# One core, Mamba layer: sums of the decay, C·B products and a logarithm moved within a pipelined step

## The reference, cut to what matters

```python
o = silu(depthwise3x3(lin1(x)))
s = o @ fc_in                                   # [b, l, 32]
z, xBC, dt = split(s @ W_in)
xs, B, C = split(silu(causal_conv4(xBC)))
dt = softplus(dt + dt_bias); dA = exp(-dt * exp(A_log))
h = dA_t * h + (dt_t * x_t) * B_t;  y_t = h @ C_t      # forward; and again on the flipped sequence
y = (y + D * xs) * silu(z)
y = y * rsqrt(mean(y * y, -1) + 1e-5) * norm_w
out = y @ W_out                                 # both directions are added, then fc_out, norm, gate
```

## Time and profile before

| what | value |
|---|---|
| median of 3 runs | 9643.34 us |
| profiled execution, its own time | 9645.11 us |
| its span | 9643.3 us |
| mean granted TensorE clock in it | 0.879 of full |
| TensorE / VectorE / ScalarE busy over the span | 76% / 69% / 60% |
| Mamba layer in the span | about 1933 to 2860 us |
| steps 17 to 31 (all three groups of blocks) | from about 2135 to 2465 us |
| steps 32 to 40 (no convolution) | from about 2468 to 2668 us |
| steps 41 to 48 (only q) | from about 2668 to 2799 us |

### The profile page before, as it was taken

The page is one execution under the profiler, slowest core; times in us unless marked ns, Lnnn a source line. Parts: engine busy times, 40 slices in busy tenths (PEclk is TensorE's granted clock), DMA queues, the critical chain, the costliest instruction groups (busy, mean ns, idle before and its releaser), DMA issues. The chain is left out here.

```text
span 9643.3 us, 117031 instructions
## 1 busy us (share of the span) xinstructions
PE 7297.0 (76%) x37876; PEld 2493.7 (26%) x37876; DVE 6652.7 (69%) x10617; ACT 5742.5 (60%) x4945; POOL 1957.9 (20%) x1578
## 2 busy tenths in 40 slices
PE   8999999968860998487666676666666676666787
PEld 3333333234430333322211122111211122111422
DVE  6777777767557333566677777877777777877565
ACT  3222232136535222322799988999799988999432
POOL 5655666400012000133000000000000000000133
PEclk9999999978875999588899998999899999999687
DMA  1000000001100000000000000000000000000000
GB/s 43 1 1 1 1 1 1 2 24 25 25 1 6 0 0 0 2 0 0 1 1 1 0 1 1 0 0 0 1 1 0 0 1 1 0 1 0 3 0 35
DMA packets 26732, 43.17 MB, mean 4 GB/s; under 512 B 13451, under 2 KB 16653, under 8 KB 25235
## 3 DMA queue, kind: packets, MB, share of 16 engines
q1 hardware_dynamic: 26386, 38.68, 1.3%
HBM read 13.49 MB, written 8.39 MB: 2 GB/s over the span
## 5 line engine op out<-in xcount | busy, mean ns | idle before, releaser
L2235 ACT ACTIVATE aa_tanh<-aa_tanh 128x4096 f32<-128x4096 f32 (+8 forms) x1280 | 3685.4, 2962 | 211.2 <-DVE aa_tanh L2404 211.2
L2404 DVE TENSOR_SCALAR aa_tanh<-aa_f_times,aa_g_bias 128x1024 f32<-128x1024 f32 (+19 forms) x5120 | 2965.5, 645 | 740.4 <-PE aa_scores L2292 735.1
L2292 PE MATMUL aa_scores<-aa_tanh,aa_w_spread 128*32 128x512 f32 (+9 forms) x18432 | 2294.0, 611 | 1352.6 <-ACT aa_tanh L2235 1350.6
L2292 PEld LDWEIGHTS aa_scores<-aa_tanh,aa_w_spread 128*32 128x32 f32 x18432 | 563.3, 115 | 3028.6 <-ACT aa_tanh L2235 2310.6
L278 POOL TENSOR_TENSOR near_tap_weights<-near_hat_y_mask,near_hat_x 128x1024 f32<-128x1024 f32 x400 | 938.1, 2366 | 468.4 <-PE near_weights_spread L570 459.8
L584 PE MATMUL near_out_sum<-near_weighted,near_w_out 128*128 128x512 f32 x1984 | 997.1, 626 | 24.0 <-DVE near_weighted L357 13.5
L570 PE MATMUL near_weights_spread<-near_tap_weights,near_spread_consts 36*64 36x512 f32 x6272 | 799.7, 610 | 19.3 <-DVE near_weighted L357 13.1
L2081 PE MATMUL L_ffn_experts<-L_ffn_expert_w,L_ffn_normed_T_block 128*128 128x512 f32 x1024 | 694.8, 766 | 152.0 <-POOL L_ffn_normed_T_block L2060 152.0
L2203 POOL COPY aa_normed_block<-aa_normed 128x128 f32 x192 | 156.9, 817 | 2726.4 <-PE aa_out_sum L2309 2726.4
L2093 ACT ACTIVATE L_ffn_weighted<-L_ffn_experts,L_ffn_logits 128x128 f32<-128x128 f32 x1024 | 292.7, 368 | 679.0 <-PE L_ffn_experts L2082 679.0
L346 DVE TENSOR_TENSOR near_weighted<-near_weights_spread,near_values 128x1024 f32<-128x1024 f32 x496 | 589.4, 1220 | 152.3 <-PE near_weights_spread L570 152.1
(11 more groups left out here) (339 smaller groups left out, 7703.8 us busy)
## 6 DMA issues: line engine op xcount, KB each, us to landing
l_taps<-l_scan_in_out SPq DMA_DIRECT2D x256, 64.0 KB, 2.0
x_rows<-in_x SPq DMA_DIRECT2D x4, 2048.0 KB, 14.2
out_x<-x_rows SPq DMA_DIRECT2D x4, 2048.0 KB, 6.3
qa_x<-in_L_attn_w SPq DMA_DIRECT2D x1, 1024.0 KB, 5.6
L_ffn_expert_w<-in_L_ffn_expert_w SPq DMA_DIRECT2D x2, 512.0 KB
near_spread_consts<-in_deform_consts SPq DMA_DIRECT2D x1, 805.5 KB, 7.5
l_weights<-in_mamba SPq DMA_DIRECT2D x1, 557.0 KB
consts_sb<-in_consts SPq DMA_DIRECT2D x1, 516.5 KB
```

Source lines behind the costliest of these rows:

```text
L2235: a.activation(TH[:, tt, 0:width], TH[:, tt, 0:width], ACT.Tanh).then_inc(th_ready, 1)
L2292: last = t.matmul(sp_[32 * q:32 * q + 32, q4, s:e], W2S[:, tt, :], TH[:, tt, o + s:o + e], start=tt == 0, stop=tt == 3, tile_position=(0, ...
L2404: last = v.tensor_scalar(TH[:, tt, at[q]:at[q] + w - s], FR[:, c * CHUNK + lo + s:(c + 1) * CHUNK], bias, None, ALU.add)
```

## The change

Three moves in `mamba_layer`, all in lists written by hand. The ring of banks, the semaphores' meanings, the VectorE list, the GpSimd list and the DMAs are unchanged.

```diff
@@ scalar @@
                 if valid(q - 1):
                     ms = bank("rms", q - 1)
-                    a.wait_ge(rms_done, 1 + q)
-                    a.activation(ms, ms, ACT.Ln, bias=C["eps5"]).then_inc(ln_ready, 1)
                     a.wait_ge(ln_ready, 1 + q)
                     a.activation(ms, ms, ACT.Exp, scale=-0.5).then_inc(rs_ready, 1)
@@ scalar, between the SiLU of the convolution and the copy of x @@
                     a.activation(O2[:, g % 2, :], O2[:, g % 2, :], ACT.Silu).then_inc(o2_ready, 1)
+                if valid(q):
+                    ms = bank("rms", q)
+                    a.wait_ge(rms_done, 1 + q + 1)
+                    a.activation(ms, ms, ACT.Ln, bias=C["eps5"]).then_inc(ln_ready, 1)
                 if valid(m):
@@ tensor, start of the step @@
                 q, m, n = g - P2, g - A2, g - 1
-                if valid(q):
-                    t.wait_ge(r_ready, 1 + 2 * q + 2)
-                    if q:
-                        t.wait_ge(gl_ready, 1 + 2 * q)
-                    for r in range(2):
-                        last = t.matmul(ps[:, CUM + r, :], ONES[:, :], R[:, r, :, :].rearrange("p c t -> p (c t)"), start=True, stop=True)
-                    last.then_inc(cum_done, 1)
                 if valid(m - 1):
@@ tensor, before the C B products @@
+                if valid(m):
+                    t.wait_ge(s4_loaded, 1 + (m + 1) * 2 * DC * 16)
+                    project(m, "B", 1, b_done)
+                    project(m, "C", 2, c_done)
                 if valid(q):
                     b, j = block_out(q)
                     t.wait_ge(tm_ready, 1 + 2 * q + 2)
@@ tensor, after the C B products @@
                     last.then_inc(g_done, 1)
-                if valid(m):
-                    t.wait_ge(s4_loaded, 1 + (m + 1) * 2 * DC * 16)
-                    project(m, "B", 1, b_done)
-                    project(m, "C", 2, c_done)
                 if valid(q - 1):
@@ tensor, end of the step @@
                     t.matmul(at[:, 2 * NC:4 * NC], ONES[:, :], AV[:, b % 2, :, :].rearrange("p r c -> p (r c)"), start=True, stop=True).then_inc(ct_done, 1)
+                if valid(q + 1):
+                    t.wait_ge(r_ready, 1 + 2 * q + 4)
+                    if q + 1:
+                        t.wait_ge(gl_ready, 1 + 2 * q + 2)
+                    for r in range(2):
+                        last = t.matmul(ps[:, CUM + r, :], ONES[:, :], R[:, r, :, :].rearrange("p c t -> p (c t)"), start=True, stop=True)
+                    last.then_inc(cum_done, 1)
```

## The result

The changed kernel takes 9670.26 us (median of 10 runs, 9661.84 to 9674.15), the kernel before, run beside it, 9643.47 us (10 runs, 9638.31 to 9656.33). The medians differ by 26.8 us; the ratio of the comparison is 1.0025, which is 24 us, with a 95% interval of 1.0015 to 1.0035 (14 to 34 us). Forecast were 21 us (9664). Nearly the whole difference lies in the Mamba layer. The profiled execution's span went from 9643.3 to 9667.5 us, and the time from the mark R of step 17 to that of step 48 from 645.0 to 665.9 us. Of all executions in this document one, of the kernel in "The ring's hold taken away from the changed kernel", took 13454.82 us at a granted clock of 0.756, where the others have 0.88, and is left out of its ratio.

The account below looks back on a forecast made before the run. VectorE was taken to bound full steps, TensorE those without convolution. 28 + 1.4 + 8.4 - 1 - 16 = +21 us, added to the median of 9643.34, gave 9664 us, 0.22% slower; range 9645 to 9683.

Parts of the forecast that it names:

- The decay sums at cost 0: TensorE's list: moving the sums from first place of a step to last of the one before changes nothing, cost 0.
- C·B behind the projections, and B held by line 1204: Full steps: B waits until line 1204 frees its bank, making line 1214 3.5 us late; +28 us over eleven.
- The absorbed stall before line 1225: VectorE before line 1225 (y-times-z): its old 0.95 us stall is absorbed, leaving net +2.55 us a step.
- Steps 24 and 32: Steps where the dt products follow y on TensorE: only y's end counts, together +1.4 us.
- Steps 17, 18, 25 and 33: Where the ring or late decay sums differ, C·B is pushed back by projections: 2.1 us each, +8.4 us.
- Steps 34 to 40: Steps without convolution: B is free early, C waits for line 1204; the order gives -1 us in seven.
- I take R+7.2, between them, as low-clock stretches ran in both: Steps 34 to 40: y starts 7.2 us after line 1192's second half starts, between 6.2 and 8.1; -0.2 us a step.
- The logarithm, "gain 0" in full steps and 1.96 us in each later one: ScalarE: no gain with convolution; without it load and Ln hide before the copy, 1.96 us eight times, -16 us.
- The main case: Whole kernel: the forecast sum of +21 us, spread over clock patterns from +12 to +32 us; chance 0.60.
- the first (the clock stays high): TensorE's clock stays high after the idle time before B: about 9638 us, no change; chance 0.14 with its mixtures.
- a granted clock off 0.89: Stretch from 2135 to 2500: a granted clock clearly off 0.89 would show the prediction wrong in its size.
- the third: TensorE: the bank hold does not bind, B and C fill the gap; -48 us, 9595 us; chance 0.04.

Follow-up runs that it names:

- The ring's hold taken away from the changed kernel: The changed kernel with line 1204 put on VectorE between the two halves of line 1192; 9625.55 us, ratio 0.9978.
- the two experiments that take it away: The changed kernel with line 1204 earlier on VectorE, 9625.55 us; the changed kernel with two products that nothing reads behind fc, 9649.46 us.

## Why the prediction was right, and where it was not

- **The decay sums at cost 0.** Shown, by the same list of instructions and a ratio of 1.000.
- **C·B behind the projections, and B held by line 1204.** Shown: B at R+1.87 for R+1.85, and at R+0.22 when line 1204 was put earlier. Line 1214 was forecast at R+6.45 and came at R+6.3 to R+6.75. The eleven steps gave +28.9 us for +28. The low clock that the forecast counted on was there in all eleven, as the two experiments that take it away show (1.8 us of line 1214's delay). Alone, this part costs 43 us, where 40 to 45 were expected. The absorbed stall before line 1225 was right too: it is 0 in all eleven.
- **Steps 24 and 32**: +0.5 for +1.4, which says nothing for or against, since the same list scattered by 3.5 us there.
- **Steps 17, 18, 25 and 33** were undersized: +13.1 us, for 8.4 less the logarithm's 2.0. Steps 17 and 18 fit; 25 and 33 gave +4.6 and +3.8 (with the logarithm's gain in the latter), against 2.1 and 0.1. In both the products came back later than priced: line 1214 is 3.1 us later after R in step 25 and 4.1 in step 33. And from the start of y to y-times-z it took 1.5 and 1.7 us more, at a granted clock of 0.67 and 0.64, where it was 1.00 in both before; for that the forecast had no term. (Step 25's figure is one to be careful with: the same list as before had line 1214 there at R+4.85 and at R+6.20.)
- **Steps 34 to 40** were undersized by more: -21.9 us, for -1 from the order and -14 from the logarithm. The step that failed is "I take R+7.2, between them, as low-clock stretches ran in both". They did not run in the new one: line 1214 is at R+4.0, and y starts at R+6.2, the fast end of the range. But this is not owed to the order on TensorE: with the old order and the logarithm moved the seven steps took 17.16 us too.
- **The logarithm, "gain 0" in full steps and 1.96 us in each later one** was right as to ScalarE and wrong as to its worth. The stall at R is 2.03 us in full steps, as before; in the later steps 1.96 us hid ahead of the copy, and 18.21 against 16.24 us at the full clock show the gain by itself. Alone the move gains 33 us. About 16 of them are the forecast's, in steps 33 to 40; some 9 more in steps 34 to 40 and 5 to 7 in full steps go with a clock that falls less often. That the fall stays away because TensorE's idle time is broken up fits the rows, and filling that idle time has the same effect; breaking it up by something other than the logarithm was not tried. Behind the projections' wait the clock's gain is lost again in full steps: there the idle times are 1.86 and 2.33 us and the clock fell all the same. So the parts don't add up: +43 and -33 alone make +10, and together they are +24 to +27.
- **The sum** was right to 3 to 6 us, and this was partly luck: two errors of some 7 us each have opposite signs. The main case is what happened in full steps. Of the rivals, the first (the clock stays high) held for steps 34 to 40 and not for full steps; the sign that the forecast gave for its size, a granted clock off 0.89, shows a little (0.86); the ring's hold, on which the third rested, was where the forecast put it.
- **The table load**: 1.28 us and the next activation 0.02 us after its end, in the changed kernel too. What was moved was worth 1.96 us of ScalarE's time: in steps 34 to 40, 0.42 of the 2.40 us of idle were left over. By the rule of the Trainium skill ("ScalarE: Activation LUTs", section "What ACT_TABLE_LOAD costs"), a load and a drain, it would have been an estimated 3.3 us; the load is as the page says, the drain does not show here.

## What to carry to other kernels

When work is moved into an idle time of an engine, ask first who frees the buffer that it writes, and where that stands in the other engine's list; here it stood behind the very wait that made the idle time, and a ring counted on paper told it before any run. An idle time of TensorE can cost twice, by itself and by a clock that falls in it or just behind it: filling it with products that nobody reads was worth 15 to 26 us, so price the clock at both levels in each stretch. Parts of a change that act through the clock can't be added; try them alone and together. And run the unchanged list a second time before reading a difference of 1 to 3 us in a single step.

## What was not expected of the hardware

- The same 3.1 us of idle time per step, cut in two by 1.7 us of light work, let the clock alternate between steps with a fall and steps without (21.1 and 19.5 us). In the changed kernel, with 1.86 and 2.33 us of idle, it fell in all eleven (line 1214 at R+6.3 or later); with 1.86 and 1.00 us it did not (20.45 us in each of the steps 27 to 31 of that kernel). The idle times alone don't decide it: with the added products step 28 of the changed kernel had a fall and its ten like steps, with the same list and the same idle time before the state products, had none; and in the kernel before, line 1214 is at R+2.42, 2.99 and 3.31 in steps 27 to 29, because the fall comes at another place of each. What exactly decides is left open.
- Where the added products did not keep the clock from falling, in step 28 of the changed kernel, they still gained, because they and not the projections ran in the slow stretch (3.33 us for two, against 1.98 at the full clock; line 1214 at R+5.79 for R+6.73).
